# Attention in a gated cross-attention stack: projections as single matmuls over sixteen slots, and another order of TensorE's work within a step

## The reference, cut to what matters

```python
q = (x @ Wq).reshape(b, n, 32, 16)            # x after layer norm, 4 batches of 512 tokens, 512 wide
k, v = jnp.split(ctx @ Wkv, 2, axis=-1)       # ctx 512 x 256
q = apply_axial_rope(q, pos_map)
k = apply_axial_rope(k, ctx_pos_map)
logits = jnp.einsum('bqhd,bkhd->bhqk', q, k) * scale
w = jax.nn.softmax(logits, axis=-1)
attn = jnp.einsum('bhqk,bkhd->bqhd', w, v).reshape(b, n, 512)
return attn @ Wout + bout                     # then x + tanh(gate) * this
```

## Time and profile before

| | us |
|---|---|
| median of 3 runs | 1495.58 (1495.02 to 1496.68) |
| the profiled execution | 1494.6 |
| its span, first to last instruction | 1493.1 |
| TensorE matmul busy | 1186.9 (79%) |
| VectorE busy | 847.4 (57%) |
| ScalarE busy | 649.5 (44%) |
| GpSimd busy | 401.5 (27%) |
| mean granted TensorE clock | 0.902 of full speed |

### The profile page before, as it was taken

One profiled execution on the slowest core, in us unless ns is written; L12 is line 12 of the kernel. 1 busy time (PEld: TensorE's weight loads), 2 busy tenths in 40 slices (PEclk: granted clock), 3 DMA queues, 4 the chain that ended last, 5 costly groups with the idle time before them and its releaser, 6 DMA issues. The chain is left out here.

```text
span 1493.1 us, 18209 instructions
## 1 busy us (share of the span) xinstructions
PE 1186.9 (79%) x5251; PEld 517.3 (35%) x5317; DVE 847.4 (57%) x1314; ACT 649.5 (44%) x1145; POOL 401.5 (27%) x474
## 2 busy tenths in 40 slices
PE   2657566679988999993337899899899999875897
PEld 2333334345544444441101222332232223222453
DVE  3585857641344555521468787667757776415534
ACT  1333232345532222226304666556746665733543
POOL 0505051411113222212453332222303320005332
PEclk8777787889998999997657999999999999996999
DMA  5141311244324444426163332222312330007011
GB/s 197 43 140 34 126 69 57 95 162 136 113 96 170 157 143 147 139 92 200 57 186 104 98 108 75 78 69 81 92 47 84 94 90 7 3 1 85 29 43 43
DMA packets 106348, 141.46 MB, mean 95 GB/s; under 512 B 20788, under 2 KB 75572, under 8 KB 106280
## 3 DMA queue, kind: packets, MB, share of 16 engines
q1 hardware_dynamic: 87912, 111.77, 23.1%
q0 software_dynamic: 18368, 28.85, 7.4%
HBM read 97.44 MB, written 46.27 MB: 96 GB/s over the span
## 5 line engine op out<-in xcount | busy, mean ns | idle before, releaser
L2223 DVE TENSOR_REDUCE a_top<-PS 128x2 f32<-128x1024 f32 x256 | 309.3, 1223 | 114.7 <-PE PS L2002 107.6
L2083 ACT ACTIVATE a_E<-PS 128x512 f32<-128x512 f32 x512 | 277.7, 597 | 134.7 <-PE PS L1985 134.6
L1985 PE MATMUL PS<-a_Q,a_K 99*128 99x512 bf16 (+1 forms) x467 | 161.3, 391 | 33.2 <-ACT a_E L2083 20.5
L1251 PE MATMUL PS<-f_W,f_GT 128*128 x312 | 142.2, 599 | 0.0
L2002 PE MATMUL PS<-a_K,a_Q 64*128 64x512 bf16 x512 | 105.0, 408 | 43.6 <-issue 19.3
L2015 PE MATMUL PS<-a_E,a_V 128*32 128x512 f32 x1024 | 138.0, 612 | 0.4 <-ACT a_E L2083 0.4
L1985 PEld LDWEIGHTS PS<-a_Q,a_K 99*128 99x128 bf16 (+1 forms) x512 | 41.5, 97 | 188.7 <-ACT a_E L2083 165.7
L1307 DVE TENSOR_TENSOR f_H<-f_SG,PS 128x256 f32<-128x256 f32 x39 | 16.4, 422 | 125.8 <-ACT f_SG L1291 125.8
L1251 PEld LDWEIGHTS PS<-f_W,f_GT 128*128 128x128 f32 x312 | 57.2, 193 | 57.5 <-issue 57.5
L1641 POOL TENSOR_TENSOR a_qf<-a_qf,a_tab 128x512 f32<-128x512 f32 x16 | 20.6, 1290 | 206.6 <-DVE a_swapped L2173 206.6
L1270 PE MATMUL PS<-f_W,f_HT 128*128 x156 | 73.3, 593 | 0.0
(11 more groups left out here) (351 smaller groups left out, 1982.1 us busy)
## 6 DMA issues: line engine op xcount, KB each, us to landing
f0r_raw<-in_L_ffn_W_dram SPq DMA_DIRECT2D x24, 512.0 KB, 5.3
a_K<-k_parts SPq DMA_DIRECT2D x192, 64.0 KB, 2.2
a_Q<-a_q_parts SPq DMA_DIRECT2D x192, 64.0 KB, 2.2
f_y<-f_Y SPq DMA_DIRECT2D x39, 256.0 KB, 2.0
v_units<-V SPq DMA_DIRECT2D x16, 512.0 KB, 3.7
a_V<-v_units SPq DMA_DIRECT2D x16, 512.0 KB, 3.5
k_parts<-f_k_parts SPq DMA_DIRECT2D x16, 384.0 KB, 3.4
a_q_parts<-a_parts SPq DMA_DIRECT2D x16, 384.0 KB, 2.6
```

What stands on the lines that cost most here:

```text
L1251: last = nc.tensor.matmul(PS[:, 2 + k % 2, 0:2 * I], GT[k][:, c, :], W13[:, bass.ds(e, 1), c, :].rearrange("p a n -> p (a n)"), start=(c = ...
L1985: nc.tensor.matmul(PS[:, 4 + h % 2, :], K6[k][0:rows_, o, head // 2, kt * P:(kt + 1) * P], Q6[k][0:rows_, o, head // 2, :], start=True, st ...
L2083: nc.scalar.activation(E[step % 2][:, h, :], PS[:, 4 + h % 2, :], ACT.Exp).then_inc(exp_done, 1)
L2223: nc.vector.tensor_reduce(top[:, h - h % 2:h - h % 2 + 2, t], PS[:, 2 * pair:2 * pair + 2, :], AX.X, ALU.max).then_inc(maxed, 1)
```

## The change

- The four matmuls of a q and of a p become four jobs of one matmul each, accumulating in the bank. Only the first waits for the bank, and only the last signals.
- The slots are given anew. q parts in slots 0 to 3 (in turn 0: 0, 0, 1, 2); o of the unit before in 4 (3); a in 6 (5); m in 9; o of the unit itself in 10 (11); x, in turn 0 only, in 6, 7, 8 and 10; p parts in 12 to 15 (13, 14, 15, 15). Each turn c of batch b projects tile c of batch b - 1.
- TensorE's order in a step becomes: two scores, slot 2s, values, two scores, both maxima pairs, slot 2s + 1.
- `attnT` becomes two buffers by batch; the second also holds four of the six row buffers of `Combine` until the last row tile is added. `attn` becomes two buffers of a unit's width.
- The normalisation of batch b + 2 is done in turn (b, 3); that of batch 0 stays in turn (-1, 0). `swap` moves from slot 2 to slot 5.
- The loop is written out. One closing turn remains, in which the last four projections go to banks 7, 4, 5 and 0 without waiting for one another.

```diff
-            if c == 1:
-                for n, when in ((2, 0), (3, 0)):
-                    add(when, "x", (b + 1, 0), n)
-            add(0, "q", before(b, c, -3))
-            if c == 1:
-                add(2, "p", (b - 1, 0), 3)
-            add(4, "o", before(b, c, 1), 1)
-            add(8, "a", before(b, c, 1))
-            add(10, "m", before(b, c, -1))
-            add(11, "o", (b, c), 0)
-            if c == 0:
-                add(12, "p", (b - 1, 0), 0)
-                add(13, "x", (b + 1, 0), 0)
-                add(14, "p", (b - 1, 0), 1)
-                add(15, "p", (b - 1, 0), 2)
-                add(15, "x", (b + 1, 0), 1)
+            if b == NB:
+                add(3, "o", before(b, c, 1), 1)
+                add(5, "a", before(b, c, 1))
+                for t in range(TB):
+                    for d in range(DC):
+                        add(8 + 2 * t + d // 2, "p", (b - 1, 0), (t, d))
+                return found
+            crowded = c == 0
+            for d, when in enumerate((0, 0, 1, 2) if crowded else (0, 1, 2, 3)):
+                add(when, "q", before(b, c, -3), d)
+            add(3 if crowded else 4, "o", before(b, c, 1), 1)
+            add(5 if crowded else 6, "a", before(b, c, 1))
+            add(9, "m", before(b, c, -1))
+            if crowded:
+                for d, when in enumerate((6, 7, 8, 10)):
+                    add(when, "x", (b + 1, 0), d)
+            add(11 if crowded else 10, "o", (b, c), 0)
+            for d, when in enumerate((13, 14, 15, 15) if crowded else (12, 13, 14, 15)):
+                add(when, "p", (b - 1, 0), (c, d))
...
+        def bank_of(kind, unit, extra):
+            return PS[:, (7, 4, 5, 0)[extra[0]], :] if kind == "p" and unit[0] == NB - 1 else PS[:, 7, :]
...
+        def batch_to_norm(b, c):
+            nb = {0: b + 1 if b == -1 else None, DC - 1: b + 2}.get(c)
+            return nb if nb is not None and is_batch(nb) else None
...
-                    for d in range(DC):
-                        last = nc.tensor.matmul(B, attnT[:, d, extra * P:(extra + 1) * P], wo[:, d, :], start=(d == 0), stop=(d == DC - 1))
-                    last.then_inc(projected, 1)
+                    last = nc.tensor.matmul(bank_of(kind, unit, extra), attnT[b % 2][:, d, t * P:(t + 1) * P], wo[:, d, :],
+                                            start=(d == 0), stop=(d == DC - 1))
+                    if is_last_part(kind, extra):
+                        last.then_inc(projected, 1)
...
+                        goes_on = {"q": lambda: extra > 0, "p": lambda: extra[1] > 0 or (unit[0] == NB - 1 and extra[0] > 0)}.get(kind, lambda: False)()
+                        if prior[0] is not None and not goes_on:
...
                     scores((b, c), step, 0)
                     scores((b, c), step, 1)
-                    maxima(*heads[step], 0)
                     slot(2 * step)
-                    scores((b, c), step, 2)
-                    scores((b, c), step, 3)
-                    maxima(*heads[step], 1)
                     if step == 0:
                         values(before(b, c, 1), 7)
                     else:
                         values((b, c), step - 1)
+                    scores((b, c), step, 2)
+                    scores((b, c), step, 3)
+                    maxima(*heads[step], 0)
+                    maxima(*heads[step], 1)
                     slot(2 * step + 1)
...
-                    at(2, swap)
+                    at(5, swap)
```

More of the change, by code:

```diff
@@ L1708, in attention @@
         rsum = sb("rsum", [P, TB, 4, 1])
-        attn = sb("attn", [P, TB, D])
-        attnT = sb("attnT", [P, DC, S])
+        attn = [sb(f"attn{k}", [P, TB, P]) for k in range(2)]
+        attnT = [sb(f"attnT{k}", [P, DC, S]) for k in range(2)]
         weights, pos, ys, ffn_gate = routed
-        rows = Combine(nc, sb, sem, X, F32, weights, pos, ffn_gate, ys, 3)
+        rows = Combine(nc, sb, sem, X, F32, weights, pos, ffn_gate, ys, 3, [attnT[1][:, d, :] for d in range(DC)])
         w_loaded = sem("w_loaded")
@@ L1789, in jobs @@
+            for d, when in enumerate((13, 14, 15, 15) if crowded else (12, 13, 14, 15)):
+                add(when, "p", (b - 1, 0), (c, d))
             return found
         def turns(eng, turn):
[L1792 to L1796, removed]
+            for b in range(-1, NB):
                 for c in range(DC):
                     turn(b, c)
-            for c in range(DC):
-                turn(NB - 1, c)
@@ L1801, in turns, with is_last_part @@
             turn(NB, 0)
-            turn(NB, 1)
+        def is_last_part(kind, extra):
+            return {"q": lambda: extra == DC - 1, "p": lambda: extra[1] == DC - 1}.get(kind, lambda: True)()
+        def bank_of(kind, unit, extra):
+            return PS[:, (7, 4, 5, 0)[extra[0]], :] if kind == "p" and unit[0] == NB - 1 else PS[:, 7, :]
         def n_unit(unit, per=1):
@@ L1966, in slot @@
                         prior[0] = job
-                if not isinstance(b, int) and c == 0:
-                    prior[0] = [j for n in range(16) for j in jobs(*before(b, c, 1), n)][-1]
-                if isinstance(b, int) and b == NB - 1 and c == 0:
-                    prior[0] = [j for n in range(16) for j in jobs(b - 1, DC - 1, n)][-1]
                 def scores(unit, step, h):
@@ L2069, in slot @@
                             act.wait_ge(a_turned, n_unit(unit))
-                            if unit[1] == 0 and not is_first(unit, DC):
-                                act.wait_ge(projected, unit[0] * TB)
-                            nc.scalar.copy(attnT[:, unit[1], :], PS[:, 7, :]).then_inc(aT_ready, 1)
+                            if unit == (1, 0):
+                                act.wait_ge(rows.tile_added, NT)
+                            if unit[1] == 0 and unit[0] >= 2:
+                                act.wait_ge(projected, (unit[0] - 1) * TB)
+                            nc.scalar.copy(attnT[unit[0] % 2][:, unit[1], :], PS[:, 7, :]).then_inc(aT_ready, 1)
                 def exps(unit, step, hs):
@@ L2094, in turn @@
                 for step in range(8):
-                    if c == 0 and step == 3 and is_batch(b + 1):
-                        act.wait_ge(var_ready, b + 2)
+                    nb = batch_to_norm(b, c)
+                    if step == 3 and nb is not None:
+                        act.wait_ge(var_ready, nb + 1)
                         nc.scalar.activation(sd[:], mv[:, :, 1], ACT.Sqrt, bias=ln_eps[:]).then_inc(sd_ready, 1)
@@ L2150, in normalize @@
                         chn.wait()
-                        if not (isinstance(nb, int) and nb == 0):
+                        if nb:
                             v.wait_ge(xT_ready, nb * DC)
```

59 lines of the change are left out of this document (31 added, 28 removed).

## The result

The changed kernel takes 1530.5 us (median of 4 runs, 1529.4 to 1532.5), the kernel before 1495.3 (4 runs, 1493.3 to 1496.7). The ratio is 1.0238 (95% interval 1.022 to 1.0256), so the change costs 35 us. I had forecast 1502, range 1480 to 1520. The direction was right. The size was not: the time lies outside the range.

A forecast was written before the change was run, and what follows sets the result against it. No engine was full, TensorE nearest, each step a 3.21 us ring of TensorE and ScalarE. Lead-in +4.8, batch 0 +1.9, batches 1 and 2 +2.0, batch 3 +1.5, end -3.3: +6.9 on 1495.58, forecast 1502, range 1480 to 1520.

The forecast's parts named there:

- Order in a step: TensorE's new order in attention steps: empty step from 3.21 to 2.88 us, step with two projection parts 4.44.
- Side jobs against VectorE: VectorE's unchanged order makes TensorE's side jobs wait in full turns; waits 5.3 us of a 35.8 us turn.
- the four waits: TensorE waits in full turns: before a 1.05, first p part 1.05, m 0.7, first q part 1.5 us.
- the low end of the unknown costs: In attention turns, none of the four waits appears, as VectorE might stand earlier: 39 us less, so 1463.
- m behind the cut: TensorE's m job in slot 9 waits 0.7 us behind VectorE's 1.5 us cut of the maxima.
- Nothing: Priced at nothing: buffer changes; also swap to slot 5, delaying GpSimd some 7 us, covered except without margin in batch 0.
- Clock: TensorE's granted clock: new waits of 0.5 to 1.5 us costed at nothing; high end +22 us over 13 turns.
- Rival 2: Regular TensorE waits lower the granted clock, under 0.97 in batches 1 to 3; +10 to +22, 1512 to 1524; chance 0.12.
- Normalisation: Moved to the preceding turn 3, 7.3 us of VectorE: turn 3 takes 38 in batch 1, 35.4 in batch 0; lead-in +4.8.
- Loop and end: Unrolling saves 0.5 us a turn; last four projections lose three waits of 1.1, -3.3.
- Rival 1, the step wins: Side jobs meet VectorE early, waits before a, p, m under 0.3 us: 1475, half of it 1488; chance 0.29.
- Rival 3, maxima rows late: GpSimd's later rotation delays rows the first score needs, 1 to 2 us in 12 turns: 1514 to 1526; chance 0.06.

The follow-up runs named there:

- experiment 2: Changed kernel, but VectorE handles an even slot's side job before reducing that slot's maxima; 1502.8 us, ratio 1.0049.
- experiment 7: Experiment 5, with VectorE also doing the add of the last slot (15) before the turn's last maxima; 1476.7 us, ratio 0.9869.
- experiment 10: Changed kernel with only GpSimd's order altered: from batch 0 on maxima rows, then next turn's row fetches, then query rotation; 1508.1 us, ratio 1.009.
- experiment 5: Experiment 2 plus, from batch 0 on, GpSimd sending maxima rows, then fetching the next turn's rows, then rotating; 1484.0 us, ratio 0.9918.
- experiment 1: Changed kernel, but GpSimd sends the maxima rows before it rotates the queries; 1517.7 us, ratio 1.0152.
- experiment 9: Kernel before, with the loop written out and the last four projections not waiting for one another; 1486.9 us, ratio 0.9948.
- experiment 3: Changed kernel with TensorE's old order in a step, all else of the change kept; 1477.5 us, ratio 0.9878.
- experiment 6: Changed kernel with the old order in a step (experiment 3) and GpSimd's order of experiment 5; 1479.7 us, ratio 0.9885.
- experiment 8: Kernel before with only the swap moved from slot 2 to slot 5; 1506.2 us, ratio 1.0062.

## Why the prediction was wrong in size

By its own steps:

- *Order in a step.* Right. Empty steps 2.88 were forecast; those without any wait take 2.77 to 2.97 (turn (3, 1)). Steps with two parts: 4.44 forecast, 4.42 measured with p parts, 4.70 with q parts.
- *Side jobs against VectorE.* Three of the four waits are right: a 1.05 forecast, 1.01 measured at 1026.69; the first p part 1.05 against 0.92; the first q part 1.5 against 1.40. Experiments 2 and 7 took most of them away, for 27.8 and 7.2 us; the low end of the unknown costs had listed 30.6 us for these three (39 with m). That end was not reached, since VectorE's program order forces the waits, as forecast.
- *m behind the cut, and "Nothing:".* This is the step that failed, with its 0.7 us for the wait before m. I took the cut's 1.5 us from the earlier trace rows, where the rotation has all but ended, priced the move of `swap` from slot 2 to slot 5 at nothing, and asked only whether GpSimd would end in time. The move puts the rotation beside the cut. The trace of the kernel before had the clue, in its timeline of the same stretch:

```profile
1020.43 1.15 POOL L1654 TENSOR_TENSOR a_parts<-a_qf,a_parts 128x512 bf16<-128x512 f32 x1
...
1021.66 0.18 DVE L2186 CAST a_mcut<-a_ntop 128x32 bf16<-128x32 f32 x1
1021.87 0.19 DVE L2188 TENSOR_TENSOR a_ntop<-a_ntop,a_mcut 128x32 f32<-128x32 f32 x1
```

The cut's first operation takes 0.51 there and the next four 0.18 to 0.19 each. That first operation ends at 1021.62, and GpSimd's last rotation operation at 1021.58; undisturbed the cut takes 1.1 (experiment 10). So even the 1.5 us that I read was a disturbed value. The lead-in turn (-1, 3) of the same trace has the collision in full, with a cut of 2.3 us (781.29 to 783.62):

```profile
782.40 1.18 POOL L1654 TENSOR_TENSOR a_parts<-a_qf,a_parts 128x512 bf16<-128x512 f32 x1
...
782.60 1.02 DVE L2192 TENSOR_TENSOR a_mcut<-a_ntop,a_mcut 128x32 bf16<-128x32 f32 x1
```

  After the change the cut takes 2.9 us, the wait before m 1.1 to 2.36 in the full turns in place of 0.7. Adding step 4 over the 13 full turns, the changed kernel is 19.6 us above experiment 10. The rest of the 22.5 is a balance that I did not take apart: the changed kernel has more drops of the clock in the batches (nine against two), experiment 10 loses 3.3 us in step 6 of turn (0, 3). Experiment 10 gives the price of the step as a whole, 22.5 us of the 28 that were missing; experiments 2 and 5, with VectorE's order mended, give 18.8.
- *Clock.* I costed nothing because the new waits were to be 0.5 to 1.5 us. At that length that held in batches 1 to 3 (experiment 10: 1.00). Seven of the nine drops follow a wait before m that had grown to 1.68 us or more. Rival 2 is thereby at most a follower: nine drops at 1.2 us would be some 11 us, an estimate, and the kernel before has three of them in the same stretch; its mark, a clock under 0.97 in batches 1 to 3, was not met (0.98, 0.98, 0.99).
- *Normalisation.* Turn (1, 3) 38.0 forecast, 38.8 without the collision. In the lead-in from VectorE's first reduction to the first exponential: +4.8 forecast, +5.7 measured (37.7 to 43.4); the first reduction itself came 2.7 us earlier in the changed kernel's trace, which no part of the change explains. It lies between 752.9 and 758.1 among the traces of all runs, and at 757.1 and 757.0 in experiments 1 and 2, which differ from the changed kernel only in the order of one engine; so it looks like the scatter of single executions.
- *Loop and end.* Right: -4 (eight turns of 0.5) and -3.3 forecast, and experiment 9 gives -8.8 for both. Its trace has 3.9 us of it in batches 1 and 2 (turns 30.1 to 29.57) and only 1.7 at the end, where its clock drops once; in the changed kernel's trace, without that drop, the end fell from 22.4 to 18.8.
- *Rival 1, the step wins,* named the right lever and the wrong state of it: it needs VectorE's order turned as well. Then it reaches 1484.0 and 1476.7, near the 1475 I gave it. But the old order reaches 1477.5 with the rest of the change (experiment 3), so no run shows the order itself gaining anything on the whole program.
- *Rival 3, maxima rows late:* not seen. The waits of the changed kernel over the attention batches have none of TensorE for a transfer of these rows.

Not settled: why the clock drops once at the end of experiment 10 (0.92 against 1.00 in the changed kernel), which makes its end 1.2 us longer than forecast, and why the same wait before m brings a drop in one turn and none in another.

## What to carry to other kernels

When a piece of work is moved on one engine, look at what the other engines do at the time it moves to, not only at whether it ends in time: VectorE and GpSimd slow each other on data outside PSUM, and a duration read beside an idle partner is not the duration beside a working one, and a first operation longer than its like (0.51 among 0.19) is the sign to look for. When TensorE's order is changed, change the order in which its partner empties the banks with it; experiment 2 did this with one condition and got 28 us. What a slow operation costs depends on who waits behind it: the same collision was worth 22 us under the one order (experiment 10), nothing under the other (experiment 6), and in the kernel before, where nobody waited for the cut itself, the move still cost 10.4 us through the reductions behind it (experiment 8).

## What the runs showed of the hardware

- Five VectorE operations on 128 x 32 numbers, 0.18 to 0.19 us each alone, took up to 1.30 beside GpSimd operations of 1.2 to 1.3 us on 128 x 512 (experiment 3). So one lost up to 1.1 us, six times its own length and a little less than one GpSimd operation. Which of the five is hit depends on the phase: on average over 15 cuts the last at 858 ns in the changed kernel, the third at 871 in experiment 8, the first cast at 672 in experiment 3.
- An addition of 128 x 512 numbers with both inputs outside PSUM, 0.74 alone, took 3.47 and 3.48 beside three GpSimd operations (experiment 1). The loss of 2.7 us is more than one of them takes, so it can be held by more than one.
- The blocking works both ways: a GpSimd operation of 1.16 took 3.06 beside a VectorE addition of 2.44.
- VectorE's reductions from PSUM kept 1220 to 1223 ns on average in all these kernels, with GpSimd beside them or not.
- In the four batches of the changed kernel, waits before m of 1.68 to 2.36 us were followed by a drop of the clock in 7 turns and not in 4 others (2.36 in three of them), so the length of that wait alone does not decide it. Experiment 10, with 0.55 in a like turn, had none in batches 1 to 3.
